# Two AdaLN transformer blocks on one core: token transposes and queries one expert step later, layer 1's LN apply up to two steps earlier

## What is computed

```python
h = _layernorm(x) * (1 + ca) + sa
x = x + ga * attn(h)
h = _layernorm(x) * (1 + cb) + sb
x = x + gb * ffn(h)
```

## Time and profile before

| | |
|---|---|
| three timed runs | 484.39, 489.24, 489.26 us, median 489.24 |
| the profiled execution | 487.31 us, of it span 485.4 us |
| busy in the span | TensorE 427.4 us (88%), VectorE 358.5 (74%), ScalarE 340.3 (70%), GpSimd 262.2 (54%) |
| mean granted TensorE clock | 0.849 |

### The profile page before, as it was taken

The page is one execution under the profiler, slowest core; times in us unless marked ns, Lnnn a source line. Parts: engine busy times, 40 slices in busy tenths (PEclk is TensorE's granted clock), DMA queues, the critical chain, the costliest instruction groups (busy, mean ns, idle before and its releaser), DMA issues.

```text
span 485.4 us, 7696 instructions
## 1 busy us (share of the span) xinstructions
PE 427.4 (88%) x2180; PEld 286.4 (59%) x2180; DVE 358.5 (74%) x884; ACT 340.3 (70%) x902; POOL 262.2 (54%) x283
## 2 busy tenths in 40 slices
PE   3799959799799899886998889979989999799995
PEld 3577856587476577552433335324448877587783
DVE  5564884666988869769868896896748777759773
ACT  2457746798687685777998789978946566575552
POOL 2351655696776776841353454434419965656663
PEclk9999988899999999986556555555579999999999
DMA  6700003121124553643048434304115442432640
GB/s 184 220 1 1 1 1 111 65 90 43 45 95 102 150 157 87 138 101 111 2 76 108 124 80 109 88 11 96 26 24 154 127 122 80 140 108 90 174 131 22
DMA packets 45218, 43.62 MB, mean 90 GB/s; under 512 B 5500, under 2 KB 33588, under 8 KB 45176
## 3 DMA queue, kind: packets, MB, share of 16 engines
q1 hardware_dynamic: 45176, 43.13, 33.8%
HBM read 36.68 MB, written 6.43 MB: 89 GB/s over the span
## 4 chain that ended last, share of the span: by engine, by line
PE 41%; DVE 13%; issue 5%; ACT 3%; POOL 1%; POOLq 0%; DVEq 0%; ACTq 0%
PE P L1189 8%; PE P L1191 8%; PE P L1190 7%; PE P L1445 7%; PE P L1435 5%; DVE nm L866 5%; PE P L1319 1%; DVE SC L600 1%; ACT EX L1124 1%; POOL hidl L463 1%; PE P L1288 1%; PE P L1205 1%; DVE P L929 1%; PE P L1313 1%; DVE kvs L691 1%
## 5 line engine op out<-in xcount | busy, mean ns | idle before, releaser
L463 POOL TENSOR_TENSOR hidl<-tmp,hidh 128x512 fp32r<-128x512 f32 x116 | 149.3, 1295 | 83.0 <-ACT hidh L1074 82.1
L1124 ACT ACTIVATE EX<-P,nm 128x256 f32<-128x256 f32 x256 | 116.9, 499 | 14.1 <-DVE nm L866 14.0
L1074 ACT ACTIVATE hidh<-tmp 128x512 fp32r<-128x512 f32 x116 | 73.0, 630 | 48.0 <-DVE tmp L829 23.2
L866 DVE TENSOR_REDUCE nm<-P 128x4 f32<-128x1024 f32 x64 | 77.9, 1219 | 23.4 <-PE P L1435 23.1
L1445 PE MATMUL P<-EX,qs 128*32 128x256 f32 x512 | 66.8, 619 | 11.8 <-DVE O L881 11.7
L1189 PE MATMUL P<-XH,WH 128*128 128x512 f32 x176 | 75.4, 429 | 1.0 <-DVE O L881 0.5
L1191 PE MATMUL P<-XL,WH 128*128 128x512 f32 x176 | 70.1, 398 | 0.0
L1190 PE MATMUL P<-XH,WL 128*128 128x512 f32 x176 | 70.1, 398 | 0.0
L507 POOL TENSOR_TENSOR qs<-qT,rz 128x128 f32<-128x128 f32 x64 | 24.5, 404 | 79.9 <-DVE rz L874 79.9
L829 DVE TENSOR_TENSOR tmp<-P,G 128x512 f32<-128x512 f32 x64 | 43.4, 687 | 31.1 <-ACT P L1095 19.0
L1435 PEld LDWEIGHTS P<-VS,KS 24*128 24x128 f32 x256 | 30.9, 290 | 49.0 <-ACT EX L1124 34.4
(11 more groups left out here) (131 smaller groups left out, 680.9 us busy)
## 6 DMA issues: line engine op xcount, KB each, us to landing
G<-gate_rows SPq DMA_DIRECT2D x56, 256.0 KB, 3.3
kv_parts<-kvs SPq DMA_DIRECT2D x16, 256.0 KB, 2.4
VS<-kv_parts SPq DMA_DIRECT2D x48, 64.0 KB
KS<-kv_parts SPq DMA_DIRECT2D x48, 64.0 KB
G<-gate_rows SPq DMA_DIRECT2D x8, 224.0 KB, 3.0
G<-gate_rows SPq DMA_DIRECT2D x8, 192.0 KB, 3.0
G<-gate_rows SPq DMA_DIRECT2D x8, 160.0 KB, 2.6
X<-in_x SPq DMA_DIRECT2D x4, 256.0 KB, 4.6
```

The costliest lines, as they stand in the source:

```text
L463: nc.gpsimd.tensor_tensor(hidl[:, u % 3, :], source, hidh[:, u % 3, :].bitcast(fp32), ALU.subtract).then_inc(s["low_ready"], 1)
L866: v.tensor_reduce(nm1[:, g % 4, 2 * h:2 * h + 2, :], P[:, bank:bank + 2, :].rearrange("p j (h s) -> p (j h) s", h=2), AX.X, ALU.max, negat ...
L1074: sc.activation(hidh[:, u % 3, :], source, ACT.Copy).then_inc(s["high_ready"], 1)
L1124: last = sc.activation(ex1(g, j)[:, h * S:(h + 1) * S], P[:, bank_s1(g, j), h * S:(h + 1) * S], ACT.Exp, bias=nm1[:, g % 4, j, h:h + 1], a ...
```

## The change

It has two parts, and no instruction is added or taken out.

Part A, in layer 0's experts of quarters 1, 2 and 3: TensorE's `transpose_tokens(2, p - 1)` moves from step 14 to 15 and `project_q(p - 1)` from 15 to 16; ScalarE's `modulate(2, p - 1)` moves from 14 to 15 and `queries_out(p - 1)` from 15 to 16. `project_kv` stays at 17.

Part B, in layer 1's experts: VectorE's `ln_apply(3, ...)` for quarters 2 and 3 moves from steps 0 and 1 of the quarter ahead of theirs to steps 11 and 12 of the quarter before that (from quarter 1 to quarter 0, from quarter 2 to quarter 1). The transposes that read it stay at step 2.

```diff
--- before.py
+++ after.py
@@ -937,14 +937,15 @@
                 v.tensor_tensor(hidf[:, n % 2, :], P[:, bank_u(n), :], G[:, q % GR, :],
                                 ALU.mult).then_inc(s["bc_read"], 1)
                 if p in (1, 2):
-                    if i in (0, 1):
-                        ln_apply(3, p + 1, i)
                     if i == 4:
                         router_logits(1, p + 1)
                     if i in (6, 8, 9):
                         router_weights(1, p + 1, (6, 8, 9).index(i))
-                if p in (0, 1) and i in (5, 7):
-                    ln_stats(3, p + 2, i // 2 - 2)
+                if p in (0, 1):
+                    if i in (5, 7):
+                        ln_stats(3, p + 2, i // 2 - 2)
+                    if i in (11, 12):
+                        ln_apply(3, p + 2, i - 11)
                 if p >= 1:
                     if i == 3:
                         gate_experts(1, p - 1)
@@ -1108,9 +1109,9 @@
                     if i == 13:
                         weights_out(0, p + 1)
                 if p >= 1:
-                    if i == 14:
+                    if i == 15:
                         modulate(2, p - 1)
-                    if i == 15:
+                    if i == 16:
                         queries_out(p - 1)
             high0(NP * STEPS0 - 1)
 
```

## The result

| | before | after |
|---|---|---|
| median of 14 runs each | 488.72 us | 483.75 us |
| lowest, highest | 484.39, 491.87 us | 477.78, 488.20 us |
| profiled execution, own time | 487.31 us | 485.78 us |
| its span | 485.4 us | 483.9 us |

The change makes the kernel about 1% faster: the ratio is 0.9894 with a 95% interval of 0.986 to 0.9928, which is 5.2 us (3.5 to 6.8). The ratio leaves out runs more than 1.5% above the fastest of their kernel; the plain means of all 14 and 14 runs, which leave nothing out, differ by 4.5 us (2.7 to 6.3). The forecast of 3.9 us lies in both.

What follows compares the result with a forecast made beforehand. TensorE was taken to bound the expert stages, so its idle time could be won: 0.9 + 3.0 = 3.9 us, giving 485.3 us from the median 489.24 and 483.6 from the mean. Forecast 484.8 us, range 480.0 to 488.2.

Steps and rivals of the forecast that it cites:

- the most likely case: Whole kernel: a change within 1% (4.9 us) of the time before, chance 0.62.
- Edit A: Layer 0, quarters 1 to 3: second attention's transposes and queries one step later, about 0.29 us each, 0.9 us together.
- the 1.46 of the view: Layer 0 quarter 1: transposes' idle wait for the router-weights copy, 1.46 us, of which only 0.28 was forecast as gained.
- The bound on the other side: Layer 0: a second ScalarE pair ahead of the modulation, 1.09 us more each quarter, would make the edit cost 2.4 us.
- Edit B: Layer 1: earlier LN apply ends the transposes' waits, 0.57 us in quarter 1 plus 2.43 in quarter 2, 3.0 us.
- The margin of 0.65 us: Layer 1 quarter 2: gated products free their banks 0.65 us before the up projections of steps 3 and 4 need them.
- The root: Layer 1 quarter 0: GpSimd's reciprocal root is ready 2.1 us before the product ahead of the apply ends; no new wait.
- (1): Layer 0: VectorE's operations stretched beside GpSimd leave edit A nothing; 484.3 us, from the median 486.2; chance 0.18.
- the prediction's error of about 1 us: Layer 0 quarter 1: shifted order of VectorE's apply and GpSimd's low parts puts about 1 us either way on 0.3.
- (2): Layer 1 quarter 2: late gate rows hold TensorE at step 4, edit B gives about 1.0 of 3.0; chance 0.12.
- (3): Attention: the earlier start loses granted clock, costing 4.9 us and leaving the kernel 1.0 us slower; chance 0.08, mirror 0.06.
- (4): Layer 0: edit A's waits vanish whole, 3.7 us, with 3.0 makes 6.7; 480.6 us, from the median 482.5; chance 0.10.

Runs made afterwards that it cites:

- e1: Kernel before with only the second attention's token transposes, modulation and queries one step later: 488.03 us, ratio 0.9991 to before.
- e7: Kernel before with the second attention's token transposes written to bank 4 instead of bank 7, no step moved: 487.39 us, ratio 0.9987 to before.
- e4: Changed kernel with the second attention's transposes, modulation and queries one step further, at 16 and 17: 482.94 us, ratio 0.9894 to before.
- e5: Changed kernel with ScalarE's modulation at step 15 ahead of that step's high-part copy: 482.34 us, ratio 0.9886 to before.
- e2: Kernel before with only layer 1's LN apply moved to steps 11 and 12 of the quarter before: 483.65 us, ratio 0.9898 to before.
- e10: Changed kernel with each moved LN apply of layer 1 done twice, the extra into an unread buffer: 483.99 us, ratio 0.9905 to before.
- e8: e4 with VectorE's LN apply for the second attention two steps later, at 12 and 13: 483.65 us, ratio 0.9905 to before.
- e9: e8 with the modulation also ahead of the high-part copy of step 16: 480.76 us, ratio 0.9860 to before.
- e6: e4 with the modulation ahead of the high-part copy of step 16: 482.27 us, ratio 0.9870 to before.
- e3: Kernel before with layer 1's whole LN apply at the head of step 0, ahead of the gate-row wait: 484.87 us, ratio 0.9900 to before.

## Why the prediction was right

The forecast was 484.8 us in a range of 480.0 to 488.2; the median is 483.75. By the ratio the gain is 1.06%, just over the 1% at which the most likely case (within 1%) was to end, and the interval reaches to both sides of it.

**Edit A, 0.29 us a quarter: measured 0.30, 0.31 and 0.29 up to the first key/value projection of each quarter** (and 0.07 more behind that of quarter 1; the shift from before falls from 3.04 to 2.07 over the three quarters; in e1 from 1.92 to 0.96). It was forecast 0.9 in sum, and is 0.97. Each piece held: one pair of ScalarE, 1.09 us between the GELU and the modulation; 142.25 - 139.93 = 2.32 us from the query to the key/value projection, as worked out; waits of 0.72 and 0.70 from start to start, where 0.7 and 0.7 were expected. e7 shows why the 1.46 of the view wasn't to be counted, e4 and e5 that the term comes from ScalarE's queue. The bound on the other side, a second pair in the way, didn't occur: the order written in the queue was the order in which ScalarE ran.

**Edit B, 0.57 + 2.43 = 3.0 us: measured 0.56 + 2.55 (e2 against before) and 0.59 + 2.25 (after against e1).** Each pair has the same pace of TensorE in the first stretch; after against before reads 0.80 there, 0.24 of it pace. In the second stretch the gain hangs on how long the apply stood behind the gate row: the transposes waited 2.28 us in before, 1.91 in e1 and 1.88 in e7. So B gives 2.8 to 3.1, with 3.0 in it. The margin of 0.65 us for the gated products of units 26 and 27 held: TensorE has no wait between steps 2 and 4 of quarter 2. The root was ready, the new place was hidden (e10), the wait for a gate row stayed (2.01) and cost nothing.

**The rivals.** (1) Stretched operations on VectorE eat A: they occurred and didn't decide. In quarter 1 the LN apply of two tiles took 1.55 and 1.49 us beside GpSimd and 0.60 at 133.25, and A still won its 0.3. The Trainium skill, GPSIMD Engine Reference, section 1 (Specifications), names contention of GpSimd with VectorE instructions in a two-port mode or with two SBUF inputs. The trace agrees in that the applies stretch (1.55 against 0.60); no row tells which mode they ran in. That A came through whole in quarter 1 is in part luck. The second key/value projection there waits for VectorE's copy in both kernels, 0.64 us before and 0.60 after, and the same wait was 0 in e4 and e8, 0.59 in e9, 0.96 in e7 and 1.14 in e6: it swings by more than the 0.3 at stake, as the prediction's error of about 1 us had allowed. (2) The next gate row in place of the first: one wait of 0.38 at 425.68, hidden. (3) The attention's clock: 0.54 against 0.53, no loss. Between the last key/value projection of layer 0 and the router weights of layer 1 the traces differ by more than edit A: e1 3.3 us longer than before, e3 2.2 shorter, after 0.1 longer. By their clock records the traces of before and of after both spend 136.5 us of it at the level of 0.50, e1 143.3 us and e3 119.5. Up to the end of this stretch e2 and e3 run the code of before, and they came out 1.4 us longer and 2.2 shorter. So swings of 2 to 3 us occur there with no edit ahead, and nothing ties them to the offset that the change makes. (4) The waits of A go whole: no, 0.97 of 3.7.

**What stays open.** The traces add up to 3.8 to 4.1 us. The ratio says 5.2, the plain means 4.5, and both intervals hold 3.9, so there is nothing that needs another cause; but B alone measured 5.0 by its ratio and 3.2 by its means, e3 4.9 and 3.8, and whether B gives a microsecond more than its two stretches show isn't settled. Chance or a weak effect of an earlier layer 1 on later stages would look the same with this spread.

## What to carry to other kernels

When a wait is about to be removed, add up what stands in the queue of the engine that makes the next input, and forecast the start of the next operation that everyone waits for, not the length of the wait: here 1.46 us of idle time were worth 0.09 (e7) and nothing over the stage, and moving the work behind it by a step 0.30. Operations that need no DMA should not be queued behind one that does: four small ones behind a wait for a gate row cost 2.2 to 2.6 us, and both places ahead of it that were tried were as good. Where an edit is worth less than the spread between runs, compare the lengths of stretches between two fixed operations of the bounding engine; edit A gave 0.97 and 0.96 us in two traces whose spans differ by 5 us. That holds where the granted clock is 1.00 throughout. Even there two traces without B differed by up to 0.57 us in layer 1's two stretches together (some 0.2 of it pace, the rest the wait behind the gate row). In the attention, where the granted clock changes within the stretch and not alike in two traces, stretches differed by up to 3.3 us from before's, and say nothing of an edit this small.

## What the runs showed of the hardware

**TensorE reached its full level 6 us later in one execution than in the other, and a 1.00 in the clock column can mean that there is no record.** In the first attention, before any changed line, the same eight matmuls in the traces of before and of after:

```profile
25.29 1.16 PE L1246 MATMUL P<-w0v,XT 128*128 128x128 f32 x8 [0.25 <-DVE ss L711]
```

```profile
25.89 2.07 PE L1247 MATMUL P<-w0v,XT 128*128 128x128 f32 x8 [0.26 <-DVE ss L711]
```

The window of 25 to 30 us of after reads 1.00 all the same:

```profile
25.00:30.00 5.00, 4.75 (x14) 3.43 (x15) 1.14 (x3) 0.96 (x2) 1.01 (x1) 1.00 0.00 0
```

But its trace has no clock record before 30.6 us, before's none ahead of 24.4, and a stretch without a record is printed as 1.00. The trace of e4 has records there. It shows the same matmuls at the same slow pace, and a granted clock of 0.50:

```profile
24.77 2.08 PE L1247 MATMUL P<-w0v,XT 128*128 128x128 f32 x8 [0.25 <-DVE ss L711]
```

```profile
23.00:29.00 6.00, 5.75 (x20) 4.31 (x19) 1.27 (x3) 2.06 (x4) 1.01 (x1) 0.50 0.00 0
```

In after the next eight of this kind, at 32.64 and so behind the first record, take 1.05 us. So 2.07 us is the level of 0.50 (1.2 GHz) and 1.05 to 1.16 that of 1.00 (2.4 GHz). That accounts for the 3 us by which the trace of after is late: from 24.4 to 30.6 us it ran at half the clock where before ran at full, an estimate of 6.2 / 2 = 3.1 us. Transposes start 0.12 us later than before's at 21.20 us and 2.91 us later at 61.72. Whoever compares two traces from the front takes such a shift for an effect of the change.

**VectorE's LN apply beside GpSimd.** Two tiles of LN apply on VectorE took 0.59 to 0.60 us beside an idle GpSimd and 0.85 to 2.56 beside a busy one (e10; 0.87 to 2.54 in after). In e10 the doubled apply is a good look at it: lines 601 and 604 do the same work twice in a row, for 0.85 and 1.68 us from 383.69 on, where GpSimd has low parts until 384.21 and again from 384.52, and for 0.59 and 0.60 from 387.40 on, where GpSimd is idle until 388.22.
